# Four sorted, truncated and attention stages of an eight-stage transformer kernel: norm factors computed a stage ahead, new order of two routing stages and of the weighings in the attentions with heads of 16

## The reference

```python
x = x + _L0_xattn_ref(_layernorm(x), ctx, ctx, ...)   # stage a0: 16 heads of 16, k and v shared by all heads
x = x + _L0_ffn_ref(_layernorm(x), ...)               # stage f0: 16 experts, top 2, plus 2 shared experts
x = x + _L1_xattn_ref(_layernorm(x), ctx, ctx, ...)   # stage a1: retention, 16 heads of 16
x = x + _L1_ffn_ref(_layernorm(x), ...)               # stage f1: 8 experts, hidden 1024, the last chosen wins
x = x + _L2_xattn_ref(_layernorm(x), ctx, ...)        # a2: 16 heads of 16, biases
x = x + _L2_ffn_ref(_layernorm(x), ...)               # f2: self-attention, 16 heads, normed q, a routed gate
x = x + _L3_xattn_ref(_layernorm(x), ctx, ctx, ...)   # stage a3: heads of 64
x = x + _L3_ffn_ref(_layernorm(x), ...)               # stage f3: 8 experts, weights truncated
```

## Time and profile before

| | us |
|---|---|
| three executions | 1851.01 (median), 1850.71, 1861.83 |
| profiled execution, its own time | 1849.09 |
| span of the profiled execution | 1847.3 |
| mean granted share of TensorE's full clock | 0.897 |
| PE, DVE, ACT, POOL busy in the span | 1464.8, 967.9, 705.8, 507.2 |
| a0; f0; a1; f1 (roughly, from the span's start) | 16 to 222; 223 to 403; 411 to 626; 628 to 863 |
| a2 with f2; a3; f3 | 869 to 1336; 1337 to 1787; 1789 to 1847 |

### The profile page before, as it was taken

One profiled execution on the slowest core, in us unless ns is written; L12 is line 12 of the kernel. 1 busy time (PEld: TensorE's weight loads), 2 busy tenths in 40 slices (PEclk: granted clock), 3 DMA queues, 4 the chain that ended last, 5 costly groups with the idle time before them and its releaser, 6 DMA issues. The chain is left out here.

```text
span 1847.3 us, 34913 instructions
## 1 busy us (share of the span) xinstructions
PE 1464.8 (79%) x12858; PEld 1158.8 (63%) x12858; DVE 967.9 (52%) x1973; ACT 705.8 (38%) x1554; POOL 507.2 (27%) x841
## 2 busy tenths in 40 slices
PE   3898684864899607996479989897679999999876
PEld 2565453653676406885346656664468999989765
DVE  2676462345666441221556667765356655665652
ACT  1465443221566401111246656664443333332111
POOL 2210027006555130001411455540033333333110
PEclk9899897887999858998789989998889999999986
DMA  4322192436775228883756534452030000000001
GB/s 136 87 71 49 36 378 83 142 120 171 176 161 121 85 97 311 309 309 126 198 113 139 131 90 113 110 116 48 8 110 7 2 8 7 8 2 2 2 7 46
DMA packets 89774, 195.54 MB, mean 106 GB/s; under 512 B 14000, under 2 KB 62512, under 8 KB 81040
## 3 DMA queue, kind: packets, MB, share of 16 engines
q1 hardware_dynamic: 76688, 172.97, 32.6%
q0 software_dynamic: 4608, 12.59, 2.1%
q10 hardware_dynamic: 8320, 7.87, 1.2%
HBM read 136.37 MB, written 57.02 MB: 105 GB/s over the span
## 5 line engine op out<-in xcount | busy, mean ns | idle before, releaser
L993 DVE TENSOR_REDUCE a_sb_mx<-a_mx 128x4 f32<-128x1024 f32 x192 | 234.8, 1223 | 117.6 <-PE a_mx L815 114.9
L736 ACT ACTIVATE a_sb_probs<-a_ex 128x512 f32<-128x512 f32 x384 | 208.7, 598 | 163.6 <-PE a_ex L836 163.1
L1399 DVE RECIPROCAL a_sb_rden<-a_ot 128x256 f32<-128x256 f32 x64 | 111.5, 1742 | 74.1 <-PE a_ot L1266 74.1
L836 PE MATMUL a_ex<-a_sb_QP,a_sb_KP 49*128 49x256 f32 x768 | 98.6, 333 | 37.2 <-ACT a_sb_probs L736 32.0
L266 POOL DMA_INDIRECT a_sb_landing<-f_y_slots,g_pos x48 | 46.3, 965 | 279.4 <-POOLq L143 266.0
L815 PE MATMUL a_mx<-a_sb_KP,a_sb_QP 48*128 48x256 f32 x768 | 89.4, 310 | 38.3 <-DVE a_sb_mx L993 26.8
L836 PEld LDWEIGHTS a_ex<-a_sb_QP,a_sb_KP 49*128 49x128 f32 x768 | 60.9, 190 | 91.4 <-issue 61.0
L849 PE MATMUL a_ot<-a_sb_probs,a_sb_v 128*32 128x256 f32 x1536 | 110.4, 408 | 2.1 <-ACT a_sb_probs L736 2.1
L1192 ACT ACTIVATE a_sb_whole<-a_gp 128x512 f32<-128x512 f32 x64 | 38.3, 598 | 178.9 <-PE a_gp L1214 177.2
L815 PEld LDWEIGHTS a_mx<-a_sb_KP,a_sb_QP 48*128 48x128 f32 x768 | 63.0, 197 | 51.2 <-DVE a_sb_mx L993 25.8
L630 POOL TENSOR_TENSOR a_sb_qs<-a_sb_qf,a_sb_qs 128x512 fp32r<-128x512 f32 x24 | 30.5, 1271 | 220.3 <-ACT a_sb_qs L694 124.4
(11 more groups left out here) (441 smaller groups left out, 3663.2 us busy)
## 6 DMA issues: line engine op xcount, KB each, us to landing
f_sb_wb<-f_w SPq DMA_DIRECT2D x20, 2052.0 KB, 10.1
a_q_moved<-a_sb_qs SPq DMA_DIRECT2D x24, 512.0 KB, 5.7
a_sb_QP<-a_q_moved SPq DMA_DIRECT2D x48, 256.0 KB, 4.3
a_k_moved<-a_sb_ks SPq DMA_DIRECT2D x16, 512.0 KB, 3.9
a_sb_KP<-a_k_moved SPq DMA_DIRECT2D x32, 256.0 KB, 5.5
a_sb_kvT<-ctxT SPq DMA_DIRECT2D x24, 256.0 KB, 3.6
a_sb_QP<-a_q_moved SPq DMA_DIRECT2D x48, 128.0 KB, 4.9
f_x_slots<-f_sb_zero SPq DMA_DIRECT2D x1, 6144.0 KB, 20.3
```

The source lines that it names most:

```text
L736: act.activation(probs[:, group % 3, 2 * (u % 2) + par], EX[par][:], ACT.Exp, scale=scale)\
L836: op = pe.matmul(EX[par][:, t, :], KP[at:at + R + 1, b % KB, u % KM, t * P:(t + 1) * P], QP[at:at + R + 1, b % 3, u, :], start=True, stop= ...
L993: dve.tensor_reduce(pair, MX[:], AX.X, ALU.max, negate=True).then_inc(mx_read, 1)
L1399: dve.reciprocal(rden[:, n], OT[n][:, 1, :])
```

## The change

1. **Norm factors.** At the end of a0, a1, a2 with f2, and a3, POOL computes the factors of batches 0 to 5 for the next stage (`factors_ahead`, after the statistics of batch 5). The next stage (f0, f1, a3, f3) leaves `norm_factors` and the square root out; before batch 6, DVE computes the factors of batches 6 and 7 (`factors_of_last`).
2. **f0.** Places are reduced and cast before everything else that is not needed for them; POOL waits for `places_known` instead of `routed`; the weights and the 48 comparisons come behind; POOL does `shared_values` of three batches, DVE of five.
3. **f1.** Places first, then four weighted row tiles, then comparisons and slots, then the other twelve tiles. SP loads the weights of the first four slots before it waits for the scatter, and their rows behind.
4. **Attentions with heads of 16.** weigh0 and weigh1 both in slot 4, weigh2 and weigh3 both in slot 0 of the next step; HEAD v from slot 5 to 6; ROUTED qT from slot 0 to slot 7 before, y from slot 0 to 2, order in slot 6 gexp, scale, v.

```diff
+AHEAD = 6
-        self.tmp = sb("ln_tmp", [P, 4, NT])
+        self.tmp = sb("ln_tmp", [P, 5, NT])
+def factors_ahead(pool, g, stats_ready, count):
+    pool.wait_ge(stats_ready, count)
+    batch_norm_factors(pool, g, 0, AHEAD - 1, g.tmp)
+def factors_of_last(dve, g):
+    arrived_norm_factors(dve, g, AHEAD, B - 1, g.tmp)
...
-HEAD_EXTRAS = {0: [("neg1", 3), ("xT", 0), ("weigh3", 4)], 1: [("q", 0), ("out1", 4)],
-               2: [("weigh0", 3), ("T0", 4), ("T1", 4)], 3: [("k", 0)], 4: [("neg0", 2), ("weigh1", 3), ("aT", 4)],
-               5: [("v", 0), ("out0", 3), ("norm", -1)], 6: [("weigh2", 3)], 7: [("y", 4)]}
-ROUTED_EXTRAS = {0: [("neg1", 3), ("qT", 1), ("xT", 0), ("weigh3", 4), ("y", 5)], 1: [("q", 0), ("out1", 4), ("norm", -1)],
-                 2: [("square", 0), ("weigh0", 3), ("T0", 4), ("T1", 4)], 3: [("k", 0), ("sums", 0)],
-                 4: [("neg0", 2), ("weigh1", 3), ("aT", 4), ("roots", 0)], 5: [("gate", 4), ("out0", 3)],
-                 6: [("weigh2", 3), ("gexp", 4), ("v", 0), ("scale", 0)], 7: [("factor", 4)]}
+HEAD_EXTRAS = {0: [("neg1", 3), ("xT", 0), ("weigh2", 4), ("weigh3", 4)], 1: [("q", 0), ("out1", 4)],
+               2: [("T0", 4), ("T1", 4)], 3: [("k", 0)], 4: [("neg0", 2), ("weigh0", 3), ("weigh1", 3), ("aT", 4)],
+               5: [("out0", 3), ("norm", -1)], 6: [("v", 0)], 7: [("y", 4)]}
+ROUTED_EXTRAS = {0: [("neg1", 3), ("xT", 0), ("weigh2", 4), ("weigh3", 4)], 1: [("q", 0), ("out1", 4), ("norm", -1)],
+                 2: [("square", 0), ("y", 5), ("T0", 4), ("T1", 4)], 3: [("k", 0), ("sums", 0)],
+                 4: [("neg0", 2), ("weigh0", 3), ("weigh1", 3), ("aT", 4), ("roots", 0)], 5: [("gate", 4), ("out0", 3)],
+                 6: [("gexp", 4), ("scale", 0), ("v", 0)], 7: [("qT", 0), ("factor", 4)]}
...
+            factors_ahead(pool, g, stats_ready, AHEAD)
...
-            norm_factors(dve, g, sqrt_in, sqrt_out)
+            if not ahead:
+                norm_factors(dve, g, sqrt_in, sqrt_out)
+                if t == AHEAD * TT and ahead:
+                    factors_of_last(dve, g)
...
+    POOL_SHARE = 3
-            with pool.Fori(0, B // 2) as b:
+            with pool.Fori(0, POOL_SHARE) as b:
                 shared_values(pool, b)
             pool.wait_ge(cleared, 16 * 2)
-            pool.wait_ge(routed, 1)
+            pool.wait_ge(places_known, 1)
...
+            for i, place in enumerate((tmp, tot)):
+                dve.tensor_tensor(place[:], pre[:], picked[:, i], ALU.mult)
+            dve.drain()
+            for i, place in enumerate((tmp, tot)):
+                dve.tensor_reduce(posf[:, i], place[:], AX.X, ALU.add)
+            dve.drain()
+            dve.tensor_copy(g.pos[0][:], posf[:]).then_inc(places_known, 1)
+
             for i in range(2):
-                dve.tensor_tensor(picked[:, i], pre[:], picked[:, i], ALU.mult)
...
+                dve.tensor_tensor(picked[:, i], picked[:, i], ex[:], ALU.mult)
             for sl in range(NS):
                 dve.tensor_scalar(cmp3[:, sl, :], tiles[:, 0, :], float(sl), None, ALU.is_le)
...
-            with dve.Fori(B // 2, B) as b:
+            with dve.Fori(POOL_SHARE, B) as b:
                 shared_values(dve, b)
...
+            for j in range(U):
+                load_expert(0, j)
+            sp.wait_ge(scattered, 16 * NT)
+            for j in range(U):
+                load_rows(0, j)
+            with sp.Fori(1, NS // U - 1) as i:
+                turn(i)
+            with last_turn(sp):
+                turn(NS // U - 1)
...
+            dve.tensor_copy(g.pos[1][:, 0, :], posf[:])
+            dve.drain()
+            weighted_rows(0, 4)
             for sl in range(NS):
                 dve.tensor_scalar(cmp3[:, sl, :], tiles[:, 0, :], float(sl), None, ALU.is_le)
...
+            dve.tensor_copy(slot[:], slotf[:]).then_inc(slots_known, 1)
+            weighted_rows(4, NT)
```

More of the change, by code:

```diff
@@ L1884, in _ @@
             def _(act):
-                norm_sqrt(act, g, sqrt_in, sqrt_out)
+                if not ahead:
+                    norm_sqrt(act, g, sqrt_in, sqrt_out)
                 for b in range(B):
@@ L2487, in _ @@
             dve.drain()
-            dve.tensor_copy(g.pos[0][:], posf[:])
+            for i in range(2):
+                dve.tensor_reduce(g.weight[:, i], picked[:, i], AX.X, ALU.add)
             dve.tensor_copy(used[:], tiles[:, 0, E - 1:E])
@@ L2834, in _, with weighted_rows @@
             dve.tensor_tensor(pre[:], pre[:], tiles[:, 2:3, :].broadcast_to([P, NT, E]), ALU.add)
+            dve.drain()
+            dve.tensor_tensor(pre[:], pre[:], win[:], ALU.mult)
+            dve.drain()
+            dve.tensor_reduce(posf[:], pre[:], AX.X, ALU.add)
+            dve.drain()
+            dve.tensor_copy(g.pos[1][:, 0, :], posf[:])
+            dve.drain()
+            def weighted_rows(first, last):
+                for t in range(first, last):
+                    dve.tensor_scalar(rows[:, t, :], g.x[:, t, :], g.mean[:, t:t + 1], rw[:, t:t + 1],
+                                      ALU.subtract, ALU.mult).then_inc(rows_ready, 1)
+            weighted_rows(0, 4)
             for sl in range(NS):
@@ L3030, in program @@
             elif s == "a3":
-                attention64(nc, g, s, w)
+                attention64(nc, g, s, w, ahead="a2" in stages)
         store_x(nc, g)
```

67 lines of the change are left out of this document (31 added, 36 removed).

## The result

The kernel after takes 1899.6 us (median of 4 executions, 1893.6 to 1901.0), the kernel before beside it 1852.1; the ratio is 1.025 with an interval of 1.022 to 1.028. Forecast were 1856 us in a range of 1833 to 1871. The forecast was wrong: the kernel is slower, and by more than the slower rival (B) had. The profiled execution has a span of 1898.7 us, 51.4 more than before.

The account below looks back on a forecast made before the run. TensorE was taken to bound the attentions, DMA f1. Terms -0.3 (norms), -6.3 (f0), -1.5 (f1), +9.6 (a0), +5.3 (a2), -3 (mixed steps), +1 (f2) gave +4.8: 1853.9 us, 1855.8 at the median; range 1833 to 1871.

Parts of the forecast that it names:

- rival (B): Attentions: new holes of 1.1 us in slots 2 and 5 let TensorE's clock fall; 1868 to 1876 us, chance 0.18.
- +1.4 us per full step: a0: slots 0 and 4 grow by 1.0 us each with paired weighings; +1.4 taken of these +2.0.
- gain 0: a0, slots 2 and 6: weighings leave, but waits for ScalarE's copy or the exps remain, so no time is saved.
- the 9.6: a0: the whole price of the new weighing order, +9.6 us over full, first, late and last steps.
- +3.3 (5.3 - 3 + 1): Third attention: a2 alone +5.3 us, mixed steps -3, f2 with y moved to slot 2 +1.
- the whole 6.3 is on the path: f0: the first scatter comes 6.3 us earlier and TensorE's next work waits for its rows, so -6.3 us.
- this cover of 5 us: f0: VectorE's bias addition, with one shared batch taken over, ends near 314.5, under the scatter's new end at 319.4.
- -1.5: f1: scatter about 2.1 us earlier, but rows queue behind all four weight loads and DMA bounds; -1.5 us taken.
- the waits for `f_sb_steps` and wq: Starts of f0, f1, a3: weight loads, not norm factors, release TensorE's or ScalarE's first work; norm factors gain only -0.3 us.
- a short DVE chain before batch 6: Ends of four stages: factors of the last batches on DVE, said to be covered as DVE is several batches ahead.
- (A): Attentions: pairs of weighings cost nothing and mixed and f2 steps gain their waits; 1831 to 1841 us, chance 0.30.
- (C): Stage starts: norm factors are on the path after all, -9 us instead of -0.3; 1847 us, chance 0.07.

Follow-up runs that it names:

- e4: Kernel after with eight unused identity turns added ahead of T0 in slot 2 of the HEAD steps; 1887.6 us, ratio 1.016.
- e1: Kernel before with only the new slot tables of part 4; 1888.1 us, ratio 1.016.
- e9: Kernel after with eight unused identity turns in slot 2 and eight in slot 5 of the HEAD steps; 1863.1 us, ratio 1.005.
- e8: Kernel after with weigh0 alone put back from slot 4 into slot 2 of the HEAD steps; 1891.7 us, ratio 1.018.
- e12: Kernel before with norm factors ahead for f0, f1, f3, new orders of f0 and f1, eight unused turns in ROUTED slot 7; 1832.6 us, ratio 0.988.
- e2: Kernel after with the slot tables of before, so parts 1 to 3 alone; 1858.0 us, ratio 1.000.
- e10: Kernel before with norm factors ahead for f0, f1, f3, new order of f1, eight unused turns in ROUTED slot 7; 1834.6 us, ratio 0.989.

## Why the prediction was wrong, point by point

**Part 4, the step that failed.** The order was priced at +1.4 us per full step, and this was right (e4: 20.5 against 18.9 to 19.1), with some luck, as the 1.4 was chosen between 0 and 2.0 without a row for it. What failed is that the slots left behind were priced "gain 0": the sum has no term for the clock. It stood only in rival (B), with too small a chance and size: half clock in "six to eight of the twenty steps of the two attentions", and against it "the holes are short and TensorE has run through waits of 1 us in full steps". The argument took single waits of 1 us in the trace of before as proof that they are harmless. The new order made two of them per step, in slots 2 and 5, and the full steps of a0 then took 22.0 to 23.4 us instead of the 20.5 of e4, and the part behind them 75.7 instead of 61.2: 53 us more at half clock, 22 us on top of the 9.6. (B)'s own sum was short too: six to eight steps at 2 to 3 us are 12 to 24 us, not 12 to 20. Both holes were named, that of slot 5 by (B) alone, as "slot 5 falls back to the pace of the exps: gain 0" priced the time of the slot and not what follows at the lower clock. For a2 with f2 the sum was +3.3 (5.3 - 3 + 1) and it was +9.3; here too the clock is lower (0.87 against 0.89). e1 and e9 together show it: e1 has 27 of a0's 31 us without the other parts, e9 takes 16 of them away with work that is thrown away. Not shown is what in the new order lets the clock fall, the waits or the mix of work in a step (e8 against e4).

The Trainium skill (TensorE: Matmul & The Clock Gate, "A second HAM failure mode: psum-queue depth-cycling") tells of a kernel whose TensorE idles briefly between groups of matmuls and goes back and forth between the two levels. The kernel after agrees (three of the four y's at 3.06 to 3.78 us behind two holes), and so does e9 (1.99 in the four full steps, holes filled); e4 does not quite, with 1.99 behind one such hole, where e8 has 3.08 to 3.78. No sum of the prediction weighed this section; its rule speaks for (B).

**Part 2.** Right: the first scatter earlier, 5.6 us of 6.3 forecast. Wrong: "the whole 6.3 is on the path", and "if this cover of 5 us went, the gain would shrink by what is over it". The cover was worked out at the pace of 6 us from one addition to the next, which the one trace of before had beside its scatter. With the lag the loop's last addition comes 62.6 us after the first scatter and not at 36, as in e9 and e12, and the stage ends 17 us later than forecast. The place, the cover of VectorE's shared batches, was named; the size was not (+10.8 instead of -6.3). In e9 and e12, without the lag, f0 is 6.7 and 5.0 us shorter than in the first trace of before, as forecast. Over many executions no gain of the part can be told (e2 against before 1.000, with the loss in a3 in it; e12 against e10).

**Part 3.** Right in mechanism: the rows wait for the weights, and the first hidden matmuls come 1.6 us sooner in the stage; -1.5 was taken. VectorE's last work ends 1.3 us sooner too, but the barrier behind it does not, and f1's length is 240.9 as before. Why, no run shows.

**Part 1.** Right for the starts of f0, f1 and a3: the waits for `f_sb_steps` and wq stand there as before. f3, for which the same wait was named, wins 1.6 all the same. Wrong for a3's other end: "a short DVE chain before batch 6, when DVE is several batches ahead of TensorE". There it is not ahead; it normalises the rows of batch 6 just when TensorE needs them. 6.8 us of chain cost 3.0 (a3 455.7 against 452.7; 455.7 to 458.7 in all traces with the chain, 451.3 to 454.5 in all without).

**The rivals.** (A) fell with e4: pairs cost their +1.4. (C) fell with the brackets of the first turns. (B) was right in that the clock falls with the new order, and was given 0.18; that it is the holes that do it is not shown.

## What to carry over

Before work is taken out of a slot, read whether the slot keeps TensorE busy, and give the sum a term for what stands behind it at 1.2 GHz, besides the idle time itself; where a hole of 1 us is left in each step of a loop, put matmuls there that no one reads, and measure. A cover worked out from one trace (a loop beside a scatter) is a cover of one execution: take a second trace of the unchanged kernel before leaning on it. A short chain of small operations on one engine is to be placed by what the next use needs, and not by the engine's mean load.
